# A two-layer graph network: x kept in SBUF and updated in place, dense loops laid out anew, sums cleared by GpSimd, shorter one-hot and destination rings

## The chip, the cores and the metric

One core of one Trainium2 chip runs the whole program. The metric is device time in microseconds of one execution. The kernel before has a median of 10818.31 us over 3 runs (10810.28 to 10887.77). The profile of one execution shows what lies between its first and its last instruction.

## What is computed

There are 12500 nodes with 128 features each and 200000 edges sorted by destination, with 16 features per edge. Three steps over the edges follow one another, each with a step over the nodes before and after it.

```python
h = jnp.maximum(_layernorm(x, axis=-1), 0.0)
x = x + _L0_gnn_ref(h, L0_gnn_W1, L0_gnn_w2, src, dst)       # pooling: e = (tanh(h @ W1.T) @ w2)[src], softmax over dst
h = jnp.maximum(_layernorm(x, axis=-1), 0.0)
x = x + _L1_gnn_ref(h, edge_index, edge_attr_16, ...)         # two transformer convolutions
# transformer_conv(x, src, dst, edge_attr, Wq, bq, ...)
q, k, v = x @ Wq + bq, x @ Wk + bk, x @ Wv + bv
e = edge_attr @ We
alpha = jnp.sum(q[dst] * (k[src] + e), axis=-1) / jnp.sqrt(C)
p = jnp.exp(alpha - segment_max(alpha, dst)[dst])
w = p / (segment_sum(p, dst)[dst] + 1e-16)
out = segment_sum((v[src] + e) * w, dst) + (x @ Ws + bs)
```

The first convolution has 8 heads of 16 and is followed by a relu, the second has one head of 128.

## The kernel before

The nodes are padded to 98 tiles of 128 rows, and the stages over the nodes work on 14 batches (`BATCHES`) of 7 tiles (`ROWS_B`). The edges form 391 blocks of 512. A block whose edges end in several node tiles is visited once for each tile, which gives 488 items. The stages run one after another, with a barrier between them:

- `prepare` builds identities, masks and the list of items. Its last steps need a row that goes to DRAM and comes back (`row_scratch`, `end_p`).
- `hidden_stage` computes relu(layernorm(x)) and the pooling scores and writes `pool_rows`. It loads x into the buffer `acc`, four batches ahead.
- `dense_stage("pool")` is the first pass over the edges. GpSimd gathers the rows of the source nodes, four gathers per block, into a ring of 8 blocks, and VectorE adds the weighed sums to `acc` in SBUF.
- `project_stage` adds the pooled sums to x, normalizes it, multiplies by the four weights at once (512 columns) and stores keys and values, skip rows and the queries split in three bf16 parts. It reads x again from DRAM into `xb` (three buffers) and writes the new x to `x1_rows`.
- `edge_stage("multi")` is the second pass over the edges (ring of 4 blocks). Its buffers `onehot` and `onehotT`, `dst` and `attr` hold 8 items (`U`), and the queries hold 4 (`QB`).
- `fold_stage` finishes the first convolution and prepares the second. It reads `skip1_rows` and `x1_rows` and writes `h2_rows`, `skip2_rows` and `query_cols`. The query is computed in two products, by Wq and then by a folded key weight.
- `dense_stage("single")` is the third pass over the edges.
- `output_stage` multiplies the sums by Wv and by the 17 rows of edge weights and bias, divides, adds `skip2_rows` and stores the output.

Each of the three passes begins with VectorE clearing `acc`, which is 128 x 14355 words. `acc` and `run_max` stay in SBUF all the time.

The order of the work is written out by hand. Each engine has a program of its own, and the engines wait for each other's semaphores. `D_["hidden"].wait(pe, n)` makes TensorE wait until batch n of h is there. `rolled` writes the steps of a loop out in full. In `project_stage`, `fold_stage` and `output_stage` TensorE transposes a batch, waits until ScalarE has copied the result to SBUF (`turned_sb`), and multiplies the same batch. Below, T stands for the seven transposes of a batch, and M for its products.

## Time and profile before

| | us |
|---|---|
| median of 3 runs | 10818.31 |
| span of the profiled execution | 7414.1 |
| difference of the two | 3404.2 |
| prepare and hidden_stage | 192 |
| first pass over the edges | 1986 |
| project_stage | 296.4 |
| second pass | 2367.6 |
| fold_stage | 278.5 |
| third pass | 2079.5 |
| output_stage | 214 |

The profile gives no time of its own for the profiled execution beyond the span from its first to its last instruction. The stages are cut at the first instruction that belongs to each.
### The profile page before, as it was taken

The numbers are of one execution on the slowest core, as the hardware profiler recorded it, in microseconds if no ns is written. First come the engines' busy times: TensorE is split into PE (matmuls) and PEld (weight loads), VectorE is DVE, ScalarE is ACT, GpSimd is POOL, SyncE is SP. The second block draws the span as 40 slices with busy tenths as digits, with TensorE's granted clock in tenths as the row PEclk, the third lists the DMA queues.
The fourth block names the chain that finished last, engine by engine and source line by source line (L and its number), as shares of the span: only waits on it lengthen the run. The fifth ranks groups of instructions, "written<-read, shape, count | busy, mean of one in ns | idle before, by whom it ended". The sixth has DMA issues, their size and how long they took to land. (4 is left out here: it accounts for less than half of the span.)

```text
span 7414.1 us, 172328 instructions
## 1 busy us (share of the span) xinstructions
PE 5718.3 (77%) x38285; PEld 4085.0 (55%) x38285; DVE 4663.7 (63%) x12926; ACT 3438.6 (46%) x8180; POOL 4576.5 (62%) x4707
## 2 busy tenths in 40 slices
PE   4555566666665688888888888856889999999998
PEld 3455555555542466666666666633555556666666
DVE  4444555555665788999999999933444555555542
ACT  3233333333443466666666666612444444444441
POOL 0777777777750477777666665502777777777630
PEclk7777878888986799999999999977999999999995
DMA  2334444444434666666655555534445555555532
GB/s 81 85 82 83 85 85 87 88 89 89 92 90 140 161 155 157 159 158 153 151 144 145 142 140 137 130 103 119 108 110 112 117 116 119 123 122 123 119 88 60
DMA packets 1267854, 861.45 MB, mean 116 GB/s; under 512 B 637234, under 2 KB 1158320, under 8 KB 1266840
## 3 DMA queue, kind: packets, MB, share of 16 engines
q1 hardware_dynamic: 1091672, 438.53, 25.3%
...
HBM read 780.46 MB, written 69.42 MB: 115 GB/s over the span
## 5 line engine op out<-in xcount | busy, mean ns | idle before, releaser
L757 POOL DMA_INDIRECT ring_multi<-kv_rows,src_cols x1564 | 1609.3, 1029 | 1029.7 <-issue 440.4
L1155 POOL DMA_INDIRECT ring_single<-h_rows,src_cols x1564 | 1482.6, 948 | 857.2 <-issue 480.3
L1155 POOL DMA_INDIRECT ring_pool<-pool_rows,src_cols x1564 | 1482.0, 948 | 678.6 <-issue 451.5
L1258 PE MATMUL ps_s_pool<-ident,row_pool 128*128 128x128 f32 x1952 | 365.1, 319 | 718.0 <-ACT row_pool L1300 716.8
L1300 ACT ACTIVATE row_pool<-ring_pool 128x520 f32 x488 | 309.1, 633 | 1162.1 <-POOLq L1146 1162.1
L958 PE MATMUL ps_e_multi<-w_edge,attrT 64*128 64x512 f32 x976 | 544.5, 638 | 331.4 <-DVE kv L847 310.9
L1222 DVE CUSTOM_DVE_ANT_0 masked_pool<-mask_pool,ps_s_pool,start_pool 128x512 f32<-128x512 bf16 x488 | 364.8, 748 | 633.4 <-PE ps_s_pool L1258 552.3
L1271 PE MATMUL ps_p_pool<-row_pool,probT_pool 128*128 128x129 f32 x3904 | 667.1, 325 | 55.2 <-DVE probT_pool L1235 54.2
L847 DVE TENSOR_TENSOR kv<-ring_multi,ps_e_multi 128x1024 f32<-128x1024 f32 x488 | 596.1, 1222 | 161.6 <-issue 124.0
L1258 PEld LDWEIGHTS ps_s_pool<-ident,row_pool 128*128 128x128 f32 x1952 | 254.1, 160 | 801.5 <-issue 764.9
L1305 ACT ACTIVATE rowT<-ps_r 128x512 f32<-128x512 f32 x488 | 291.7, 598 | 816.4 <-PE ps_r L1265 816.4
L1271 PEld LDWEIGHTS ps_p_pool<-row_pool,probT_pool 128*128 128x128 f32 x3904 | 602.7, 235 | 97.5 <-DVE probT_pool L1235 97.2
L1222 DVE CUSTOM_DVE_ANT_0 masked_single<-mask_single,ps_s_single,start_single 128x512 f32<-128x512 bf16 x488 | 364.7, 747 | 427.8 <-PE ps_s_single L1253 424.3
L948 PE MATMUL ps_p_multi<-message_multi,onehot 128*128 128x136 f32 x3904 | 584.2, 297 | 0.5 <-issue 0.4
L1271 PE MATMUL ps_p_single<-row_single,probT_single 128*128 128x145 f32 x3904 | 581.1, 292 | 2.4 <-DVE probT_single L1235 2.4
L1253 PE MATMUL ps_s_single<-edge_tail,cols_tail 17*128 17x512 f32 x976 | 549.7, 643 | 0.0
L948 PEld LDWEIGHTS ps_p_multi<-message_multi,onehot 128*128 128x128 f32 x3904 | 536.7, 207 | 0.9 <-issue 0.7
L1271 PEld LDWEIGHTS ps_p_single<-row_single,probT_single 128*128 128x128 f32 x3904 | 525.2, 194 | 3.6 <-DVE probT_single L1235 2.8
L1251 PE MATMUL ps_s_single<-rowT,cols 128*128 128x512 f32 x976 | 512.2, 607 | 1.5 <-issue 1.5
L1230 DVE SCALAR_TENSOR_TENSOR acc<-acc,factor_single,ps_p_single 128x145 f32 x488 | 178.9, 367 | 521.0 <-PE ps_p_single L1271 513.4
L1265 PEld LDWEIGHTS ps_r<-ident,row_single 128*128 128x128 f32 x1952 | 207.9, 142 | 493.1 <-issue 255.7
L1300 ACT ACTIVATE row_single<-ring_single 128x512 f32 x488 | 304.2, 623 | 294.5 <-POOLq L1146 292.0
...
## 6 DMA issues: line engine op xcount, KB each, us to landing
dst_pool<-in_dst_rows SPq DMA_DIRECT2D x488, 128.0 KB
dst_multi<-in_dst_rows SPq DMA_DIRECT2D x488, 128.0 KB
dst_single<-in_dst_rows SPq DMA_DIRECT2D x488, 128.0 KB
query_multi<-query_parts SPq DMA_DIRECT2D x488, 96.0 KB
cols<-query_cols SPq DMA_DIRECT2D x488, 64.0 KB
ring_pool<-pool_rows,src_cols POOLq DMA_INDIRECT x1564
ring_multi<-kv_rows,src_cols POOLq DMA_INDIRECT x1564
ring_single<-h_rows,src_cols POOLq DMA_INDIRECT x1564
```

The costliest lines, as they stand in the source:

```text
L757: pool.indirect_dma_start(out=ring[:, u, j, :], out_offset=None, in_=rows, in_offset=bass.IndirectOffsetOnAxis(ap=g.src_cols[:, c:c + 1], ...
L847: V.tensor_tensor(out=kv[:, u1 % 4], in0=in_ring(items.block(m1), 0, 2 * D).rearrange("p j (a c) -> p j a c", a=2), in1=ps_e[:].rearrange( ...
L948: i = T_.matmul(ps_p[:, 0:acc_w], lhs, rhs, start=(j == 0), stop=(j == J - 1))
L958: T_.matmul(ps_e[:], attrT[:, u % 2], w_edge[:].rearrange("k j c -> k (j c)"), start=True, stop=True).then_inc(E["edge"].sem, 1)
L1155: pool.indirect_dma_start(out=ring[:, u, j, :], out_offset=None, in_=rows, in_offset=bass.IndirectOffsetOnAxis(ap=g.src_cols[:, c:c + 1], ...
L1222: V.tensor_tensor_reduce(out=masked[:, p], in0=mask[:, p], in1=ps_s[p][:], scale=1.0, scalar=start[:, p], op0=ALU.add, op1=ALU.min, accum_ ...
L1251: T_.matmul(ps_s[p1][:], cols[:, u1 % QB], rowT[:, p1], start=True, stop=False)
L1253: T_.matmul(ps_s[p1][:], cols_tail[:, u1 % QB], edge_tail[:, u1], start=False, stop=True)\
L1258: i = T_.transpose(ps_s[p1][:, j * P:(j + 1) * P], row[:, u1, j, D + 1:D + 2].to_broadcast([P, P]), g.ident[:])
L1271: i = T_.matmul(ps_p[p3][:, 0:acc_w], probT[:, p3, j], row[:, u3, j, 0:acc_w], start=(j == 0), stop=(j == J - 1))
L1300: S_.activation(row[:, u, :, 0:copied], in_ring(items, u, 0, copied), ACT.Copy)\
L1305: S_.activation(rowT[:, u % 2], ps_r[u % 2][:], ACT.Copy).then_inc(E["rowT_sb"].sem, 1)
```

## The change

- x is loaded once, in `prepare`, into a new buffer `x_rows` that keeps all 98 tiles in SBUF. The 14 loads stand on the sync engine's queue ahead of the stores and loads of `row_scratch`. `project_stage`, `fold_stage` and `output_stage` update it in place. The loads of x and of `x1_rows` and `skip2_rows` and the stores to these two are gone. The output is stored from `x_rows`.
- GpSimd clears `acc`: all of it in `hidden_stage`, and batch by batch (1015 words per partition) in `project_stage` and `fold_stage`, as soon as VectorE has read the sums. VectorE's clear at the start of each pass is gone.
- In the three node stages TensorE now transposes batch n before it multiplies batch n - 1, and the transposed batch has two buffers. VectorE prepares batch n + 1 before it evacuates batch n - 1.
- In `fold_stage` Wq and the folded key weight are multiplied once, ahead of the loop, so that a batch's product by Wq alone and the copy `qT` between the two are gone. Skip rows are loaded up to three batches ahead.
- In `output_stage` the seven tails of 17 columns are transposed together (119 columns), and the second product of each tile takes all 119 rows with a weight matrix that is zero outside its own 17 rows. The products go to two PSUM buffers of a batch each, and semaphores count batches where they counted tiles.
- In the second pass `onehot` and `onehotT` hold 6 items (`OB`) and `dst` holds 4.
- `dst_cols`, which nothing read, and its transposes in `prepare` are gone.

The core of the diff:

```diff
+OB = 6
...
+        g.x_rows = sb(g, ctx, "x_rows", [P, NODE_TILES, D])
+        g.x_loaded = [sem(g, f"x_loaded{k}") for k in range(BATCHES // 2)]
...
+            for n in range(BATCHES):
+                sp.dma_start(g.x_rows[:, n * ROWS_B:(n + 1) * ROWS_B], rows_of(t["x"], n)).then_inc(g.x_loaded[n // 2], 16)
...
+        @block.gpsimd
+        def _(pool):
+            pool.memset(g.acc[:], 0.0)
...
-            for n in range(BATCHES):
-                D_["stats"].wait(sp, n - LOADS)
-                sp.dma_start(acc[:, n * ROWS_B:(n + 1) * ROWS_B, 0:D], rows_of(t["x"], n))\
-                  .then_inc(loaded[n % LOADS], 16)
...
-        onehot = sb(g, ph, f"onehot_{kind}", [P, U, J, P], BF16)
-        onehotT = sb(g, ph, f"onehotT_{kind}", [P, U, J, P], BF16)
+        onehot = sb(g, ph, f"onehot_{kind}", [P, OB, J, P], BF16)
+        onehotT = sb(g, ph, f"onehotT_{kind}", [P, OB, J, P], BF16)
...
-            dst = sb(g, ph, "dst_multi", [P, U, EDGES_B], U16)
+            dst = sb(g, ph, "dst_multi", [P, QB, EDGES_B], U16)
...
-                    E["rel"].wait(sp, n - U)
-                    sp.dma_start(dst[:, u], t["dst_rows"][ds(b, 1), :].to_broadcast([P, EDGES_B]))\
+                    E["rel"].wait(sp, n - QB)
+                    sp.dma_start(dst[:, u % QB], t["dst_rows"][ds(b, 1), :].to_broadcast([P, EDGES_B]))\
...
-            V.memset(g.run_max[:], -BIG)
-            V.memset(g.acc[:], 0.0).then_inc(g.acc_clear, 1)
+            V.memset(g.run_max[:], -BIG).then_inc(g.acc_clear, 1)
...
-                    E["edge_max"].wait(act, n - U)
-                    S_.activation(onehotT[:, u].rearrange("p j n -> p (j n)"), apart[:, u % 2], ACT.Relu,
+                    E["edge_max"].wait(act, n - OB)
+                    S_.activation(onehotT[:, n % OB].rearrange("p j n -> p (j n)"), apart[:, u % 2], ACT.Relu,
                                   scale=-1.0, bias=one[:]).then_inc(E["onehotT_sb"].sem, 1)
...
@@ project_stage @@
+        @block.gpsimd
+        def _(pool):
+            for n in range(BATCHES):
+                D_["x_sum"].wait(pool, n)
+                pool.memset(acc[:, n * ROWS_B:(n + 1) * ROWS_B, :], 0.0)
+            pool.memset(acc[:, NODE_TILES:SLOTS, :], 0.0)
...
+            def summed(n):
+
+                u = n % 2
+                sums = acc[:, n * ROWS_B:(n + 1) * ROWS_B, :]
+                V.tensor_scalar(den[:, u].unsqueeze(2), sums[:, :, D:D + 1], 1e-30, None, ALU.max)\
+                 .then_inc(D_["den"].sem, 1)
+                D_["den"].wait(dve, n)
+                V.reciprocal(den[:, u], den[:, u]).then_inc(D_["extra"].sem, 1)
+                D_["extra"].wait(dve, n)
+                for j in range(ROWS_B):
+                    x1 = xr[:, n * ROWS_B + j]
+                    i = V.scalar_tensor_tensor(out=x1, in0=sums[:, j, 0:D], scalar=den[:, u, j:j + 1], in1=x1,
+                                               op0=ALU.mult, op1=ALU.add)
+                i.then_inc(D_["x_sum"].sem, 1)
...
+            summed(0)
...
+                if has(k - 1, BATCHES):
+                    rest(k - 1, 0)
+                if has(n + 1, BATCHES):
+                    summed(n + 1)
+                if has(k - 1, BATCHES):
+                    rest(k - 1, 1)
...
         def _(pe):
             pe.wait_ge(s_wdve, 1)
-            for n in range(BATCHES):
-                D_["hidden"].wait(pe, n)
-                D_["turned_sb"].wait(pe, n - 1)
-                for j in range(ROWS_B):
-                    i = T_.transpose(ps_h[:, j], h[:, n % 2, j], ident[:])
-                i.then_inc(D_["turned"].sem, 1)
-                D_["turned_sb"].wait(pe, n)
-                for j in range(ROWS_B):
-                    i = n * ROWS_B + j
-                    evac.wait(pe, i - 6)
-                    T_.matmul(ps_z[i % 6][:], hT[:, j], w[:].rearrange("p a n -> p (a n)"),
-                              start=True, stop=True).then_inc(D_["product"].sem, 1)
+            for n in range(BATCHES + 1):
+                if has(n, BATCHES):
+                    D_["hidden"].wait(pe, n)
+                    D_["turned_sb"].wait(pe, n - 1)
+                    for j in range(ROWS_B):
+                        i = T_.transpose(ps_h[:, j], h[:, n % 2, j], ident[:])
+                    i.then_inc(D_["turned"].sem, 1)
+                k = n - 1
+                if has(k, BATCHES):
+                    D_["turned_sb"].wait(pe, k)
+                    for j in range(ROWS_B):
+                        i = k * ROWS_B + j
+                        evac.wait(pe, i - 6)
+                        T_.matmul(ps_z[i % 6][:], hT[:, k % 2, j], w[:].rearrange("p a n -> p (a n)"),
+                                  start=True, stop=True).then_inc(D_["product"].sem, 1)
 
...
@@ fold_stage @@
-            def step(n, u):
-                D_["hidden"].wait(pe, n)
-                D_["turned_sb"].wait(pe, n - 1)
-                for j in range(ROWS_B):
-                    i = T_.transpose(ps_h[:, j], h[:, u, j], ident[:])
-                i.then_inc(D_["turned"].sem, 1)
-                D_["turned_sb"].wait(pe, n)
-                D_["query_done"].wait(pe, n - 1)
-                for a, b in halves:
-                    i = T_.matmul(flat(ps_q, a, b), wq[:], flat(hT, a, b), start=True, stop=True)
-                i.then_inc(D_["q_turned"].sem, 1)
-                D_["product_read"].wait(pe, n - 1)
-                for j in range(ROWS_B):
-                    i = T_.matmul(ps_z[:, j], hT[:, j], ws[:], start=True, stop=True)
-                i.then_inc(D_["product"].sem, 1)
-                D_["q_turned_sb"].wait(pe, n)
-                for a, b in halves:
-                    T_.matmul(flat(ps_c, a, b), folded[:, 0:D], flat(qT, a, b), start=True, stop=True)
-                    i = T_.matmul(flat(ps_q, a, b)[0:TAIL], folded[:, D:ACC_W], flat(qT, a, b), start=True, stop=True)
-                i.then_inc(D_["folded"].sem, 1)
-            rolled(pe, BATCHES, 2, 0, step)
+            T_.matmul(ps_q[:, 0:2].rearrange("p a n -> p (a n)")[:, 0:ACC_W], wqT[:], folded[:], start=True, stop=True)
...
+            for n in range(BATCHES + 1):
+                if has(n, BATCHES):
+                    D_["hidden"].wait(pe, n)
+                    D_["turned_sb"].wait(pe, n - 1)
+                    for j in range(ROWS_B):
+                        i = T_.transpose(ps_h[:, j], h[:, n % XB, j], ident[:])
+                    i.then_inc(D_["turned"].sem, 1)
+                k, v = n - 1, (n - 1) % 2
+                if has(k, BATCHES):
+                    D_["turned_sb"].wait(pe, k)
+                    D_["q_turned_sb"].wait(pe, k - 1)
+                    for a, b in halves:
+                        i = T_.matmul(flat(ps_q, a, b)[0:TAIL], both[:, D:ACC_W], flat(hT[:, v], a, b), start=True, stop=True)
+                    i.then_inc(D_["q_turned"].sem, 1)
+                    D_["query_done"].wait(pe, k - 1)
+                    for a, b in halves:
+                        i = T_.matmul(flat(ps_c, a, b), both[:, 0:D], flat(hT[:, v], a, b), start=True, stop=True)
+                    i.then_inc(D_["folded"].sem, 1)
+                    D_["product_read"].wait(pe, k - 1)
+                    for j in range(ROWS_B):
+                        i = T_.matmul(ps_z[:, j], hT[:, v, j], ws[:], start=True, stop=True)
+                    i.then_inc(D_["product"].sem, 1)
...
@@ output_stage @@
-        sT = sb(g, ph, "sT", [P, ROWS_B, P])
-        tT = sb(g, ph, "tT", [TAIL, ROWS_B, P])
+        sT = sb(g, ph, "sT", [P, 2, ROWS_B, P])
+        tT = sb(g, ph, "tT", [TAILS, 2, P])
...
+            for j in range(ROWS_B):
+                sp.dma_start(wt[j * TAIL:j * TAIL + EDGE_DIM, j], t["L1_gnn_We1"]).then_inc(s_w, 16)
+                sp.dma_start(wt[j * TAIL + EDGE_DIM:(j + 1) * TAIL, j], row_of(t["L1_gnn_bv1"])).then_inc(s_w, 16)
...
+                    for j in range(ROWS_B):
+                        T_.transpose(ps_h[:, j], acc[:, n * ROWS_B + j, 0:D], ident[:])
+                    T_.transpose(ps_t[n % 2][0:TAILS, 0:P], tail[:, n % 2].rearrange("p t c -> p (t c)"), ident[:])\
+                      .then_inc(D_["turned"].sem, 1)
+                k, v = n - 1, (n - 1) % 2
+                if has(k, BATCHES):
+                    if k == 0:
+                        pe.wait_ge(s_w, 16 * (1 + 2 * ROWS_B))
+                    D_["turned_sb"].wait(pe, k)
+                    evac.wait(pe, k - 2)
+                    for j in range(ROWS_B):
+                        T_.matmul(ps_z[v][:, j], sT[:, v, j], wv[:], start=True, stop=False)
+                        i = T_.matmul(ps_z[v][:, j], tT[:, v], wt[:, j], start=False, stop=True)
+                    i.then_inc(D_["product"].sem, 1)
```

VectorE in the middle of `project_stage`, before (`den`, `xb`, `stat`, `agg` belong to the sums and the layernorm of a batch, `parts` and `out` to the queries and the evacuated products):

```order
L1423 SCALAR_TENSOR_TENSOR xb<-acc,den,xb 128x128 [waits dense_extra,x_loaded1]
L1423 SCALAR_TENSOR_TENSOR xb<-acc,den,xb 128x128 x6
L1428 BN_STATS stat<-xb 128x6 [waits dense_x_sum]
L1428 BN_STATS stat<-xb 128x6 x6
L1432 BN_AGGR agg<-stat 128x2 [waits dense_stats]
L1432 BN_AGGR agg<-stat 128x2 x6
L1409 TENSOR_TENSOR out<-out,parts 128x7x128 [waits dense_part]
L1438 RECIPROCAL rstd<-std 128x7 [waits dense_std]
L1441 SCALAR_TENSOR_TENSOR drift<-agg,rstd 128x7 [waits dense_hidden,dense_rstd]
L1448 TENSOR_TENSOR out<-ps_z,b_qkvs 128x512 [waits dense_product,kv_stored0]
L1448 TENSOR_TENSOR out<-ps_z,b_qkvs 128x512 [waits dense_product] x6
L1409 TENSOR_TENSOR out<-out,parts 128x7x128 [waits dense_part]
```

and in the changed kernel:

```order
L1426 SCALAR_TENSOR_TENSOR drift<-agg,rstd 128x7 [waits dense_hidden,dense_rstd]
L1415 TENSOR_TENSOR out<-out,parts 128x7x128 [waits dense_part]
L1392 TENSOR_SCALAR den<-acc 128x7
L1395 RECIPROCAL den<-den 128x7 [waits dense_den]
L1399 SCALAR_TENSOR_TENSOR x_rows<-acc,den,x_rows 128x128 [waits dense_extra]
L1399 SCALAR_TENSOR_TENSOR x_rows<-acc,den,x_rows 128x128 x6
L1404 BN_STATS stat<-x_rows 128x6 [waits dense_x_sum]
L1404 BN_STATS stat<-x_rows 128x6 x6
L1408 BN_AGGR agg<-stat 128x2 [waits dense_stats]
L1408 BN_AGGR agg<-stat 128x2 x6
L1415 TENSOR_TENSOR out<-out,parts 128x7x128 [waits dense_part]
L1439 TENSOR_TENSOR out<-ps_z,b_qkvs 128x512 [waits dense_product,kv_stored2]
```

The wait for the load of x is gone, and the summing of the next batch stands between the scale of one batch and the evacuation of the batch before it.

TensorE in the middle of `fold_stage`, before:

```order
L1625 MATMUL ps_h<-ident,h 128x128 [waits dense_turned_sb,dense_hidden]
L1625 MATMUL ps_h<-ident,h 128x128 x6
L1630 MATMUL ps_q<-hT,wq 128x512 [waits dense_query_done,dense_turned_sb]
L1630 MATMUL ps_q<-hT,wq 128x384
L1634 MATMUL ps_z<-ws,hT 128x128 [waits dense_product_read]
L1634 MATMUL ps_z<-ws,hT 128x128 x6
L1638 MATMUL ps_c<-qT,folded 128x512 [waits dense_q_turned_sb]
L1639 MATMUL ps_q<-qT,folded 17x512
L1638 MATMUL ps_c<-qT,folded 128x384
L1639 MATMUL ps_q<-qT,folded 17x384
```

and in the changed kernel:

```order
L1654 MATMUL ps_h<-ident,h 128x128 [waits dense_turned_sb,dense_hidden]
L1654 MATMUL ps_h<-ident,h 128x128 x6
L1661 MATMUL ps_q<-hT,wq_folded 17x512 [waits dense_q_turned_sb,dense_turned_sb]
L1661 MATMUL ps_q<-hT,wq_folded 17x384
L1665 MATMUL ps_c<-hT,wq_folded 128x512 [waits dense_query_done]
L1665 MATMUL ps_c<-hT,wq_folded 128x384
L1669 MATMUL ps_z<-ws,hT 128x128 [waits dense_product_read]
L1669 MATMUL ps_z<-ws,hT 128x128 x6
```

Between the transposes of a batch and the product that needs them now stand the products of the batch before, and the two products from `qT` are gone.

TensorE in the middle of `output_stage`, at the change from the transposes to the products, before:

```order
L1740 MATMUL ps_h<-ident,sums 128x128
L1741 MATMUL ps_tail<-ident,sums 17x128
L1746 MATMUL ps_z<-wv,sT 128x128 [waits dense_product_read,dense_turned_sb]
L1747 MATMUL ps_z<-wt,tT 128x128
L1746 MATMUL ps_z<-wv,sT 128x128 [waits dense_product_read]
L1747 MATMUL ps_z<-wt,tT 128x128
```

and in the changed kernel:

```order
L1762 MATMUL ps_h<-ident,acc 128x128 [waits dense_turned_sb,dense_acc_read]
L1762 MATMUL ps_h<-ident,acc 128x128 x6
L1763 MATMUL ps_tail<-ident,sums_tail 119x128
L1772 MATMUL ps_z<-wv,sT 128x128 [waits dense_product_read,dense_turned_sb]
L1773 MATMUL ps_z<-wt,tT 128x128
L1772 MATMUL ps_z<-wv,sT 128x128
```

The single transposes of the tails have become one, the transposes read `acc` itself, and the wait before each tile's products stands once in a batch.

## Rows read from the trace of the kernel before

**Rows 1.** Windows: PE, PEld, DVE, ACT, POOL busy (count), PEclk, DMA share, GB/s.

```profile
0.00:192.00 192.00, 76.78 (x339) 63.35 (x339) 91.39 (x484) 56.61 (x118) 2.46 (x15) 0.71 0.29 82
192.00:2178.00 1986.00, 1216.67 (x7808) 1090.44 (x7808) 1078.37 (x2930) 709.74 (x1465) 1482.03 (x1564) 0.84 0.41 86
2178.00:2474.40 296.40, 147.87 (x294) 64.48 (x294) 153.09 (x481) 94.56 (x169) 0.00 (x0) 0.68 0.47 143
2474.40:4842.00 2367.60, 1981.00 (x19032) 1451.11 (x19032) 2137.07 (x5860) 1544.89 (x4393) 1609.32 (x1564) 0.95 0.60 147
4842.00:5120.50 278.50, 145.10 (x464) 77.78 (x464) 78.48 (x102) 49.28 (x56) 0.00 (x0) 0.71 0.41 120
5120.50:7200.00 2079.50, 1968.11 (x9760) 1209.04 (x9760) 1077.14 (x2930) 959.65 (x1952) 1482.64 (x1564) 0.98 0.53 115
7200.00:7414.00 214.00, 182.81 (x588) 128.80 (x588) 48.13 (x141) 23.87 (x28) 0.00 (x0) 0.53 0.21 61
```

**Rows 2.** The timeline in project_stage; start us, us, engine, operation [idle before].

```profile
2195.19 1.73 PE L1460 MATMUL ps_h<-ident,h 128*128 128x128 f32 x7 [18.50 <-ACT h L1494]
2197.92 8.62 PE L1466 MATMUL ps_z<-w_qkvs,hT 128*128 128x512 f32 x14 [1.01 <-ACT hT L1502]
...
2308.18 0.95 ACT L1480 ACTIVATE parts<-out 128x896 bf16<-128x896 f32 x1 [1.16 <-DVE out L1409]
...
2321.72 2.80 ACT L1494 ACTIVATE h<-xb,drift,rstd 128x128 f32<-128x128 f32 x7 [0.99 <-DVE drift L1441]
...
2316.37 1.93 DVE L1423 SCALAR_TENSOR_TENSOR xb<-acc,den,xb 128x128 f32<-128x128 f32 x7 [7.91 <-DMA xb<-in_x]
...
2463.29 0.36 SPq L1385 DMA_DIRECT2D kv_rows<-out  x1
```

**Rows 3.** The timeline in fold_stage, TensorE and VectorE.

```profile
4866.29 0.99 PE L1625 MATMUL ps_h<-ident,h 128*128 128x128 f32 x7
4869.96 1.74 PE L1630 MATMUL ps_q<-hT,wq 128*128 128x512 f32 x4 [2.69 <-ACT query_tail L1658]
4871.54 1.72 PE L1634 MATMUL ps_z<-ws,hT 128*128 128x128 f32 x14
...
4889.26 3.29 PE L1630 MATMUL ps_q<-hT,wq 128*128 128x512 f32 x4 [2.69 <-ACT query_tail L1658]
...
4880.97 0.25 DVE L1585 TENSOR_SCALAR den<-acc 128x56 f32<-128x56 f32 x1 [16.83 <-DMA x<-x_rows]
...
4885.68 1.08 DVE L1610 TENSOR_TENSOR x<-x,ps_z 128x896 f32<-128x896 f32 x1
```

**Rows 4.** The timeline in output_stage, TensorE.

```profile
7267.19 0.79 PE L1746 MATMUL ps_z<-wv,sT 128*128 128x128 f32 x2 [1.79 <-ACT tT L1757]
...
7268.63 0.80 PE L1746 MATMUL ps_z<-wv,sT 128*128 128x128 f32 x2
...
7386.16 0.49 PE L1746 MATMUL ps_z<-wv,sT 128*128 128x128 f32 x2 [1.79 <-ACT tT L1757]
...
7386.99 0.49 PE L1746 MATMUL ps_z<-wv,sT 128*128 128x128 f32 x2
```

**Rows 5.** The timeline of VectorE at the start of the second edge stage.

```profile
2478.78 12.02 DVE L814 MEMSET acc<- 128x14355 f32 x1 [2.94 <-issue]
2491.20 1.22 DVE L847 TENSOR_TENSOR kv<-ring_multi,ps_e_multi 128x1024 f32<-128x1024 f32 x1 [0.40 <-DVE acc L814]
```

**Rows 6.** The timeline in prepare, GpSimd and VectorE.

```profile
2.09 0.50 POOL L265 MEMSET fresh_row<- 1x488 f32 x1
...
31.84 1.62 DVE L335 TENSOR_SCALAR passed<-iota_f,end_p 98x488 f32<-98x488 f32 x4
```

**Rows 7.** The window while hidden_stage loads x.

```profile
52.00:54.00 2.00, 0.47 (x1) 0.18 (x1) 0.43 (x2) 0.00 (x0) 0.00 (x0) 0.50 1.13 319
```

**Rows 8.** The timeline at the end of the second edge stage.

```profile
4809.78 0.35 SPq L793 DMA_DIRECT2D dst_multi<-in_dst_rows  x1
...
4819.05 0.72 ACT L1012 ACTIVATE apart_multi<-dst_multi,node_ids 128x512 f32<-128x512 uint16 x1
```

416 lines of the change are left out of this document (191 added, 225 removed).

## The prediction

> **What bounds the kernel now.** I read the windows by stage first, since a share over the whole span mixes stages with different limits. [rows 1] The three passes over the edges take 6433 of 7414 us. In the first, GpSimd's gathers are busy 1482 of 1986 us, TensorE 61%; the ring is filled at GpSimd's pace. In the second VectorE is busy 90% of the time. In the third TensorE is busy 95% at a clock of 0.98. The three stages between them are different: in project_stage, fold_stage and output_stage, 789 us together, VectorE is busy for about half the time or less, and the DMA share is 0.21 to 0.47. These stages wait. The timelines say for what. In project_stage VectorE waits 7.91 us for a load of x in each batch [rows 2], in fold_stage up to 16.83 us for the load of x1 [rows 3], and in output_stage TensorE stands 1.79 us in each batch until ScalarE has copied the transposed sums, and runs at a clock of 0.53 though it is busy 85% of the time [rows 1, 4]. The gain has to come from these 789 us. In the passes the change can only win or lose something at the start, or in the rings.
>
> The median of the runs is 3404 us above the span. The profile does not show what lies there. I take it as constant: predicted time = 10818 minus what the span loses.
>
> **project_stage.** Now: 296.4 us [rows 1]. The load is gone, so what is late next? In the new order evacuating batch k - 1 on VectorE is followed by ScalarE's first part of the queries (0.95), by its seven activations for batch k + 1 (2.80), by T on TensorE (1.73), by M of batch k (8.62 for 14 passes), and by the last evacuation (0.7, an estimate from VectorE's 153.09 us of work); with 0.1 to 0.2 us at each hand-over that is 15.0 us [rows 2]. The two TensorE terms are from a batch after a long idle time. If TensorE stays warm, T costs 0.99 and M 6.5 (four passes over 2 x 896 columns took 1.74, so 14 passes of 512 columns take 14 x 0.46) [rows 3], and the period is 12.3. VectorE has some 10.9 us of work in a batch (153.09 / 14) [rows 1], so it does not bind. TensorE's idle time in the new period is about 4.8 us; after 2.69 us of idle the same product took 1.74 us once and 3.29 us another time [rows 3]. I take 14. The first batch's M started at 2197.92, 20 us into the stage; now it stands behind T of batch 1, which comes 4.6 us later, so batch 0 is evacuated at 20 + 4.6 + 8.6 + 0.7 = 34 us. Then 12 periods of 14 = 168, the last M without a T before it 7, and from the last evacuation (the store at 2463.29) to the end 11 us as now. Sum 220, so **76 us less**. Ends: 12.3 gives 97 less; 17 (hand-overs and a late clock together) gives 40 less.
>
> **fold_stage.** Now: 278.5 us. TensorE's work in a batch, warm: T 0.99, the tail 1.74, the main product 1.74, the skip product 1.72, together 6.2 [rows 3]; the third query product is gone. VectorE's in a batch lasts from 4880.97 to 4886.76, 5.8 us [rows 3]. The skip rows are loaded two batches ahead, and one batch moves 1.44 MB (three transfers of 459 KB and one of 61 KB); at the 319 GB/s that the load of x reached [rows 7] that is 4.5 us. So three things lie close together, TensorE last, and nothing in the loop waits for a store that it has just issued. I take 6.8 a batch. The first two batches run at half clock: 1.73 + 3.29 + 3.29 and 1.72 lengthened to about 2.8, 11.1 each. Weights, the extra product ahead of the loop and the first hidden batch put T of batch 1 at about 15 us (estimate, from 5.8 us of VectorE's work and the weights' landing as now). The last store lands some 7.5 us after the last product. 15 + 22 + 12 x 6.8 + 7.5 = 126, so **152 us less**. Ends: 6.2 a batch gives 159 less; a TensorE at half clock throughout gives 15 + 14 x 11.1 + 7.5 = 178, 101 less.
>
> **output_stage.** Now: 214 us, 15.2 a batch. Four passes take 1.44 us at half clock and 0.83 us at full clock, 0.36 and 0.208 a pass [rows 4]. In fold_stage 14 passes of the same size took 1.72 us, 0.123 a pass [rows 3]. The difference is that here passes with 128 rows of weights alternate with passes with 17. With 119 rows I expect both to be loaded alike and the price of fold_stage: 28 x 0.123 + 8 transposing passes x 0.14 = 4.6 a batch at full clock, 8.0 at half. VectorE's 3.4 a batch (48.13 / 14) [rows 1] and ScalarE's copies hide under it. The first M waits for 15 small loads, of which the sync engine issues one in about 0.4 us [rows 2], so it starts at about 9.3. 9.3 + 2 x 8.0 + 12 x 4.6 + 5 for the last evacuation and store = 85.5, **128 us less**. The clock is the open question: it was 0.53 at 85% busy. But these passes streamed their 128 columns in 0.21 of 0.36 us, and half of them used 17 rows; the third pass, with dense work, has 0.98 [rows 1]. Ends: half clock throughout, 9.3 + 14 x 8.0 + 5 = 126, 88 less; half clock with the dear passes, 9.3 + 14 x 12 + 5 = 182, 32 less.
>
> The Trainium skill ("TensorE: Matmul & The Clock Gate", Part 3, What overlaps and what doesn't) says that a weight load overlaps running matmuls only when the row group differs. By that rule 119 rows would still conflict with 128. The trace disagrees so far: fold_stage's passes all have 128 rows and cost 0.123 [rows 3], those that change between 128 and 17 cost 0.208 [rows 4].
>
> **The clears.** VectorE's clear takes 12.02 us on record at the start of each pass [rows 5]. In the first pass the gathers set the pace from the first one on, and they do not wait for VectorE: nothing gained. The third pass begins the same way: nothing. In the second VectorE is the bound and its first real work started 0.40 us after the clear [rows 5]; the data it needs is ready some 3 us earlier, so **3 us less** (between 0 and 12). GpSimd's own clears, at 0.50 us for 488 words [rows 6], take 1.04 us for a batch and 15 us for all of `acc`; GpSimd is otherwise idle in these stages [rows 1]. If VectorE stood still for each of them, that would be 28 x 1.04 + 15 = 44 us.
>
> **prepare.** The 14 loads of x, 6.4 MB, take 20 us at 319 GB/s [rows 7], and the row that goes to DRAM and back now queues behind them. VectorE used the returned row at 31.84 [rows 6]; with loads from 9 us to about 31 it comes at about 38. hidden_stage gets 1 us back, since x is already there. **5 us more** (between 1 less and 20 more).
>
> **The rings.** On the sync engine the wait for `dst` (4 items back) comes after the wait for the queries, which is also 4 items back and comes later in ScalarE's and TensorE's order. So `dst` was in fact issued 4 ahead already: the last one went out at 4809.78 and was used at 4819.05 [rows 8]. The one-hots are last read three items after they are written, and 6 slots leave three more. Nothing.
>
> **Sum.** 76 + 152 + 128 + 3 - 5 = 354 us. Span 7414 - 354 = 7060, time 10818 - 354 = **10464**.
>
> **Rivals.**
> (a) TensorE stays at half clock in the three stages. For it: output_stage's 0.53. Against: fold_stage's products of 512 columns did run at full clock in one of its batches [rows 3]. Project 64 less, fold 101, output 88, with 3 and -5 that is 251: 10567.
> (b) The 119-row passes stay dear at full clock: 28 x 0.208 + 1.1 = 6.9 a batch, 24 a batch for the two cold ones together, 121 in all, 35 us worse: 10499.
> (c) VectorE is locked out while GpSimd clears: 44 us worse, 10508. No row shows GpSimd and VectorE side by side in such stages. The Trainium skill ("SBUF — State Buffer", Who interferes with whom) says that copies and scalar operations in their fast form and a GpSimd instruction block each other wholly. By it fold_stage would suffer most, because VectorE is nearly the bound there.
> (d) What lies outside the span is not constant but grows with the span (10818 / 7414 = 1.46): 354 x 1.46 = 517 less, 10301.
> (e) Slower: six one-hot slots are too few, and ScalarE's two activations for the next item (0.72 each [rows 8]) come to stand behind TensorE's last reading instead of beside it: 488 x 1.44 = 703 us more, 10464 + 703 = 11167. It turns the sign from 0.73 us an item on (354 / 488). Against it: the three items of slack, some 14 us at 4.9 us an item.
>
> **How the numbers follow.** Forecast 0.55, (a) 0.18, (b) 0.08, (c) 0.07, (d) 0.07, (e) 0.02, and 0.03 for a gain that the unseen 3404 us swallow. About 1% is what a measurement of this kernel can tell from no change. The best of the stage ends are 97 + 159 + 133 + 3 + 1 = 393, 10425; I go on to 10390 toward (d). At the other end (a) with project_stage at its worst and 20 us in prepare makes 40 + 101 + 88 - 20 = 209, 10609; I take 10620. This leaves out (d), (e), the swallowed gain and a tenth of the rest. All but (e) and the swallowed gain are faster by over 1%: 0.95, within 1% 0.03, slower 0.02.
>
> **What would show each step.** project_stage near 220 us with a period of 12 to 15 and no DMA as a releaser on VectorE; fold_stage near 126 with TensorE busy over 85% and a clock above 0.9; output_stage near 86, its passes at 0.12 us; the memset gone from VectorE; prepare and hidden_stage near 197; the three passes within 10 us of now. I am wrong if a node stage shows half clock, if its stores hold up VectorE, or if the second pass moves by more than 20 us.

## The result and the profile after

| | runs | median, us | range |
|---|---|---|---|
| before | 4 | 10814.3 | 10789.0 to 10887.8 |
| changed | 4 | 10518.6 | 10499.7 to 10561.6 |

The ratio is 0.971, with a 95% interval of 0.967 to 0.975: 296 us less, and from the interval 269 to 356. The prediction was 10464, 354 less.

The first surprise is the span. The profiled execution of the changed kernel took 10499.7 us and its span is 10497.8, so next to nothing lies outside. These are its windows by stage, in the order and with the columns of [rows 1]: prepare and hidden_stage, first pass, project, second pass, fold, third pass, output.

```profile
0.00:203.60 203.60, 77.13 (x326) 62.94 (x326) 95.28 (x472) 56.48 (x118) 14.51 (x16) 0.71 0.29 78
203.60:3150.60 2947.00, 1353.02 (x7808) 1217.99 (x7808) 1057.75 (x2928) 699.76 (x1464) 1477.30 (x1564) 0.71 0.26 58
3150.60:3364.90 214.30, 126.98 (x294) 62.96 (x294) 159.43 (x481) 94.49 (x169) 13.38 (x15) 0.73 0.44 138
3364.90:7075.20 3710.30, 2619.19 (x19032) 1957.85 (x19032) 2217.94 (x5859) 1539.47 (x4393) 1522.05 (x1564) 0.72 0.37 94
7075.20:7188.80 113.60, 85.96 (x415) 51.28 (x415) 78.28 (x104) 39.85 (x42) 13.38 (x15) 0.90 0.60 180
7188.80:10394.60 3205.80, 2504.89 (x9760) 1500.62 (x9760) 1058.52 (x2930) 951.65 (x1952) 1476.96 (x1564) 0.80 0.32 75
10394.60:10497.80 103.20, 67.30 (x504) 64.25 (x504) 33.79 (x141) 15.20 (x28) 0.00 (x0) 0.90 0.23 64
```

Read it in two halves. The three stages over the nodes went from 296.4, 278.5 and 214.0 us [rows 1] to 214.3, 113.6 and 103.2. The three passes, which the change hardly touches, seem to have grown from 6433 to 9863 us. In the first pass VectorE is busy 1058 us (1078 before), ScalarE 700 (710) and GpSimd 1477 (1482). TensorE is busy for longer, since its granted clock is lower: 1968 us became 2505 in the third pass (clock 0.98, now 0.80), and 1981 became 2619 in the second (0.95, now 0.72) [rows 1]. The node stages show no such loss of clock (0.73, 0.90 and 0.90 here). In the third pass 537 of the 1126 us that it grew by are TensorE's own, and the rest are waits. Here is what ended the waits of one line of the first and third pass (VectorE adding the sums to `acc`), in us and times. The largest part ends in "remote", a release that the profile does not see.

```profile
  remote: 1114.7, 204
  PE ps_p_single L1265: 343.0, 246
  issue: 238.0, 126
  PE ps_p_pool L1265: 173.5, 195
```

A comparison of two profiles must first ask whether they were taken under the same conditions. The experiments answer that.

Now the node stages. In project_stage (the timeline of TensorE) a batch takes 13.66 us, from one T to the next; TensorE waits 4.46 us before T for ScalarE's h.

```profile
3239.82 1.75 PE L1451 MATMUL ps_h<-ident,h 128*128 128x128 f32 x7 [4.46 <-ACT h L1489]
3241.36 7.66 PE L1459 MATMUL ps_z<-w_qkvs,hT 128*128 128x512 f32 x14
...
3253.48 1.75 PE L1451 MATMUL ps_h<-ident,h 128*128 128x128 f32 x7 [4.46 <-ACT h L1489]
```

In fold_stage, again in TensorE's timeline, the third line of [rows 3] stands again, at 1.72 us, and nothing is left in front of it but 0 to 1 us of waiting for VectorE's h. A batch takes 5.7 to 6.8 us.

```profile
7135.76 0.98 PE L1654 MATMUL ps_h<-ident,h 128*128 128x128 f32 x7 [0.94 <-DVE h L1609]
7136.68 1.68 PE L1661 MATMUL ps_q<-hT,wq_folded 128*17 128x512 f32 x4
7138.28 1.77 PE L1665 MATMUL ps_c<-hT,wq_folded 128*128 128x512 f32 x4
7139.89 1.72 PE L1669 MATMUL ps_z<-ws,hT 128*128 128x128 f32 x14
```

VectorE's timeline says why h is late: in the second half of the loop VectorE itself waits for the load of the skip rows, 9.0 us in 8 batches.

```profile
7161.05 1.09 DVE L1607 TENSOR_TENSOR h<-h,skip 128x896 f32<-128x896 f32 x1 [1.10 <-DMA skip<-skip_rows]
```

In output_stage the products with 119 rows follow one another at 0.11 to 0.12 us a pass (two passes from 10465.12 to 10465.35), where [rows 4] had 0.208. But there is a new wait of 2.25 us in 12 of the 14 batches, on VectorE's copy of the tails.

```profile
10464.19 0.99 PE L1762 MATMUL ps_h<-ident,acc 128*128 128x128 f32 x7 [2.25 <-DVE sums_tail L1735]
...
10465.12 0.39 PE L1772 MATMUL ps_z<-wv,sT 128*128 128x128 f32 x2
10465.35 0.39 PE L1773 MATMUL ps_z<-wt,tT 119*128 119x128 f32 x2
...
10470.66 1.76 PE L1762 MATMUL ps_h<-ident,acc 128*128 128x128 f32 x7 [2.25 <-DVE sums_tail L1735]
```

### The profile page after: what moved, and what is told of

Read it like the earlier page. It is cut to its first block and busy times, and to the rows that moved or that the text cites. A ratio compares the mean times of both kernels' runs of the same rounds, so it can differ in the third digit from the quotient of the medians.

```text
span 10497.8 us, 171974 instructions
## 1 busy us (share of the span) xinstructions
PE 6834.5 (65%) x38139; PEld 4917.9 (47%) x38139; DVE 4701.0 (45%) x12914; ACT 3396.9 (32%) x8166; POOL 4517.6 (43%) x4738
## 5 line engine op out<-in xcount | busy, mean ns | idle before, releaser
L953 PE MATMUL ps_e_multi<-w_edge,attrT 64*128 64x512 f32 x976 | 739.1, 847 | 829.2 <-ACT attrT L1033 502.5
L1285 ACT ACTIVATE prob_pool<-masked_pool,low_pool 128x512 f32<-128x512 f32 x488 | 352.2, 722 | 2222.4 <-DVE low_pool L1216 1905.9
L1265 PE MATMUL ps_p_single<-row_single,probT_single 128*128 128x145 f32 x3904 | 738.2, 344 | 259.6 <-DVE probT_single L1229 213.9
L1265 PEld LDWEIGHTS ps_p_single<-row_single,probT_single 128*128 128x128 f32 x3904 | 662.7, 237 | 290.6 <-DVE probT_single L1229 238.8
L943 PE MATMUL ps_p_multi<-message_multi,onehot 128*128 128x136 f32 x3904 | 765.5, 359 | 1.3 <-issue 1.2
L943 PEld LDWEIGHTS ps_p_multi<-message_multi,onehot 128*128 128x128 f32 x3904 | 727.1, 269 | 1.1 <-issue 1.0
L1224 DVE SCALAR_TENSOR_TENSOR acc<-acc,factor_pool,ps_p_pool 128x129 f32 x488 | 170.4, 349 | 1164.2 <-remote 901.0
L953 PEld LDWEIGHTS ps_e_multi<-w_edge,attrT 64*128 64x128 f32 x976 | 183.1, 233 | 970.0 <-ACT attrT L1033 790.4
L989 PE MATMUL ps_q_multi<-query_multi,onehotT_multi 128*128 128x128 bf16 x5856 | 578.3, 272 | 0.0
L1229 DVE COPY probT_single<-ps_t_single 128x512 f32<-128x512 f32 x488 | 336.2, 689 | 439.1 <-remote 353.3
```

The costliest lines, as they stand in the source:

```text
L943: i = T_.matmul(ps_p[:, 0:acc_w], lhs, rhs, start=(j == 0), stop=(j == J - 1))
L953: T_.matmul(ps_e[:], attrT[:, u % 2], w_edge[:].rearrange("k j c -> k (j c)"), start=True, stop=True).then_inc(E["edge"].sem, 1)
L989: i = T_.matmul(ps_q[:, j], onehotT[:, n % OB, j], query[:, u % QB, k, 0:D], start=(k == 0), stop=(k == 2))
L1229: V.tensor_copy(probT[:, p1].rearrange("p j n -> p (j n)"), ps_t[p1][:])\
L1265: i = T_.matmul(ps_p[p3][:, 0:acc_w], probT[:, p3, j], row[:, u3, j, 0:acc_w], start=(j == 0), stop=(j == J - 1))
L1285: S_.activation(prob[:, p2], masked[:, p2], ACT.Exp, bias=low[:, p2], scale=-1.0)\
```

## The experiments

All twelve runs, in the order in which they ran. They fell on three chips, and the chip turned out to matter more than any edit.

**The kernel before, once more.** No edit.

> The kernel before, unchanged, profiled once more. The earlier profile of it had a span of 7414 us, while its runs take 10818 us; the profile of the changed kernel has a span of 10497.8 us for a time of 10499.7 us, so nothing lies outside the span there. Theory A: the 3404 us lie inside the three passes over the edges, and the stages over the nodes are as in the profile at hand: project_stage 296 us, fold_stage 278, output_stage 214, prepare and hidden_stage 192, each within 5 us, the three passes together about 9830 us instead of 6433. Theory B: everything is stretched alike, by 1.46: project_stage 432, fold_stage 406, output_stage 312. Theory C (the one in the prediction): span 7414 again, and the rest outside it.

Measured: 7410.4 us for the whole execution, with a span of 7408.6. Seven further runs on this chip have a median of 7403.9. Its first pass and project_stage:

```profile
191.10:2175.10 1984.00, 1228.09 (x7808) 1098.96 (x7808) 1082.21 (x2930) 709.56 (x1464) 1480.77 (x1564) 0.83 0.40 86
2175.10:2470.70 295.60, 146.47 (x294) 64.11 (x294) 152.90 (x481) 94.59 (x169) 0.00 (x0) 0.68 0.47 143
```

None of the three theories had it: the span is again near 7414, as in C, but nothing lies outside. The 7414 us were the time of the kernel on a chip like this one, and the 10818 us that of another chip.

**TensorE's order of before in the three node stages.**

```diff
 # TensorE, in project_stage; the same in fold_stage and output_stage
-                k = n - 1
+                k = n
                 if has(k, BATCHES):
                     D_["turned_sb"].wait(pe, k)
```

> The changed kernel with TensorE's order of before in the three stages over the nodes: the products of batch n follow the transposes of batch n, behind ScalarE's copy of them. All the rest stays. In the changed kernel these stages last 214 us (project), 113.7 (fold) and 103.3 (output). Theory A: the order is what hides the copy. Then fold_stage gets 14 x 1.3 = 18 us longer (132), project_stage 14 x 1.3 to 2.5 = 18 to 35 us longer (232 to 249). In output_stage TensorE already waits 2.25 us a batch for VectorE's copy of the tails, which stands behind the evacuation; the old order trades it for a wait of 1.8 us for ScalarE's copies, so output_stage stays within 7 us of 103. Theory B: the gain came from the loads and products that are gone, not from the order: all three stages within 5 us of now.

Measured: 7057.9 us, ratio to before 0.953 (0.951 to 0.955). Project, fold and output:

```profile
2186.50:2386.20 199.70, 123.88 (x294) 57.25 (x294) 153.01 (x481) 90.57 (x169) 13.44 (x16) 0.81 0.47 148
4750.70:4888.70 138.00, 95.06 (x415) 53.59 (x415) 79.07 (x104) 37.85 (x42) 13.39 (x15) 0.85 0.50 148
6967.40:7056.40 89.00, 62.22 (x504) 59.17 (x504) 33.76 (x141) 15.20 (x28) 0.00 (x0) 0.93 0.26 75
```

Both theories fall in part. fold_stage gets 24 us longer: there the new order hides the copy. project_stage gets 15 us shorter and output_stage 14 to 16 us shorter: there the new order costs time. TensorE in project_stage shows why:

```profile
2288.86 1.70 PE L1451 MATMUL ps_h<-ident,h 128*128 128x128 f32 x7
2291.57 7.27 PE L1459 MATMUL ps_z<-w_qkvs,hT 128*128 128x512 f32 x12 [1.01 <-ACT hT L1497]
2300.51 1.13 PE L1459 MATMUL ps_z<-w_qkvs,hT 128*128 128x512 f32 x2 [1.67 <-DVE out L1439]
...
2303.41 5.42 PE L1459 MATMUL ps_z<-w_qkvs,hT 128*128 128x512 f32 x12 [1.01 <-ACT hT L1497]
```

M of batch n waits 1.01 us for the copy, but then it runs while VectorE is still summing. By the time VectorE evacuates, the six PSUM buffers are full, and the seven evacuations go back to back in 4.26 us. In the changed kernel M of batch n - 1 stands behind T of batch n, which waits for h. VectorE then evacuates in step with TensorE, one tile in 0.86 us. The period here is 11.84 us between the two lines shown, 11.8 to 13.5 over ten batches and 12.8 on average, not 13.66. In output_stage TensorE waits 1.17 us in a batch for ScalarE's copies in place of 2.25 for the tails, and a batch takes 5.44 us instead of 6.47.

**Three things of before, each in its own stage.** Narrow tails in output_stage, VectorE's clears, and x loaded late.

```diff
-            pool.memset(g.acc[:], 0.0)          # and GpSimd's clears in project_stage and fold_stage
+            V.memset(g.acc[:], 0.0)             # VectorE, at the start of each pass
...
-                        i = T_.matmul(ps_z[v][:, j], tT[:, v], wt[:, j], start=False, stop=True)
+                        i = T_.matmul(ps_z[v][:, j], tT[:, v, j], wt[:], start=False, stop=True)
...
+            # the 14 loads of x now stand here, behind the loads of end_p and jump_p
             sp.wait_ge(s_load, 96)
```

> The changed kernel with three things of before, each read in its own stage. (1) output_stage transposes and multiplies the 17-column tails one by one, with 17 rows of weights. Theory A (price of alternating between 128 and 17 rows, 0.208 us a pass at full clock and 0.36 at half, instead of the 0.108 and 0.21 now measured): 28 x 0.1 = 2.8 us more a batch at full clock, 4.2 at half, and dearer transposes, so 103 becomes 145 to 175 us. Theory B (the gain was only the loads and the order): within 10 us of 103. (2) VectorE clears acc at the start of each pass, GpSimd nothing. Theory A (GpSimd's clears cost VectorE nothing): project_stage and fold_stage within 3 us of 214 and 113.7, and the first product of keys in the second pass 8 to 12 us later. Rival (VectorE is locked out during a clear): both stages 13 us shorter. (3) x is loaded behind the row that goes to DRAM and back. Theory A: VectorE uses the returned row at 32 us instead of 39.6, and hidden_stage begins at 48 instead of 56.3, but waits some 4 us for its first x. Rival: the later begin was not due to the loads; it stays at 56.

Measured: 7187.4 us, ratio 0.971 (0.969 to 0.973). Second pass and output_stage, and TensorE inside the latter:

```profile
2387.00:4802.00 2415.00, 2007.70 (x19032) 1478.70 (x19032) 2138.90 (x5859) 1543.86 (x4393) 1598.75 (x1564) 0.94 0.58 144
6988.70:7179.60 190.90, 155.85 (x588) 113.86 (x588) 33.14 (x141) 23.86 (x28) 0.00 (x0) 0.60 0.12 35
```
```profile
7062.79 0.49 PE L1755 MATMUL ps_z<-wv,sT 128*128 128x128 f32 x2
7063.21 0.48 PE L1756 MATMUL ps_z<-wt,tT 17*128 17x128 f32 x2
...
7067.28 0.79 PE L1756 MATMUL ps_z<-wt,tT 17*128 17x128 f32 x2
7068.00 0.80 PE L1755 MATMUL ps_z<-wv,sT 128*128 128x128 f32 x2
```

(1) Passes that alternate between 128 and 17 rows cost 0.21 us again at full clock (0.42 for two) and 0.36 at half. output_stage becomes 191 us, worse than I expected, because its clock falls to 0.60 as well. The width of the weights, together with the joint transpose of the tails that this edit also takes back, is worth 86 of the stage's 109 us of gain. (2) Without GpSimd's clears project_stage and fold_stage stay at 214.7 and 114.5 us: they hold nobody up there. In hidden_stage it is otherwise. In the changed kernel (the first two lines, from its run on the slower kind of chip below) a multiplication on VectorE that takes 0.21 us without the clear (the third line, from this run) lasts until the clear ends, 8.08 us.

```profile
57.16 12.07 POOL L434 MEMSET acc<- 128x14355 f32 x1 [53.94 <-POOLq L197]
61.22 8.08 DVE L460 TENSOR_SCALAR w2b<-w2b 128x128 f32<-128x128 f32 x1
...
53.85 0.21 DVE L456 TENSOR_SCALAR w2b<-w2b 128x128 f32<-128x128 f32 x1
```

(3) VectorE uses the returned row at 29.6 us instead of 39.6 and hidden_stage begins at 47.3 instead of 56.3. The second pass, though, is 50 us longer than in any other kernel, which needed runs of its own.

**Two orders moved further.**

```diff
 # VectorE, output_stage
-                if has(n + 1, BATCHES):
-                    divisors(n + 1)             # copies the tails
+                if has(n + 2, BATCHES):
+                    divisors(n + 2)
 # VectorE, project_stage: rstd and drift (scale) of batch n + 1 ahead of the evacuation
+                if has(n + 1, BATCHES):
+                    scale(n + 1)
                 if has(k, BATCHES):             # evacuates batch k = n - 1
 # ScalarE, project_stage
+                if has(n + 1, BATCHES):
+                    hidden(n + 1)
                 if has(k, BATCHES):
                     part(k, 0)
```

> The changed kernel with two orders moved further. In output_stage VectorE copies the tails two batches ahead instead of one, so that the transposes no longer wait behind its evacuation. In project_stage VectorE computes scale and drift of batch n + 1, and ScalarE h of batch n + 1, ahead of the evacuation of batch n - 1. Theory A: in output_stage the 2.25 us of idle TensorE in each batch go, 103.3 becomes 74 to 80 us; in project_stage the 4.46 us of idle TensorE go and VectorE's own work of 10.9 us is the period instead of 13.66, so 214 becomes 175 to 185. Together 55 to 68 us less than the changed kernel, 0.6%. Rival: another limit is close behind (stores, ScalarE, or a clock at half), and each stage gains less than 10 us.

Measured: 7008.6 us, ratio 0.947 (0.945 to 0.949). Project and output, and VectorE and TensorE:

```profile
2191.40:2382.90 191.50, 120.92 (x294) 56.12 (x294) 152.71 (x481) 94.67 (x169) 13.40 (x15) 0.79 0.49 154
6937.50:7006.80 69.30, 60.44 (x504) 59.67 (x504) 33.76 (x141) 15.20 (x28) 0.00 (x0) 0.91 0.34 96
```
```profile
2290.82 4.27 DVE L1445 TENSOR_TENSOR out<-ps_z,b_qkvs 128x512 f32<-128x512 f32 x7
...
6962.09 0.93 PE L1775 MATMUL ps_h<-ident,acc 128*128 128x128 f32 x7
...
6966.09 0.93 PE L1775 MATMUL ps_h<-ident,acc 128*128 128x128 f32 x7
```

output_stage is 34 us shorter, more than expected: TensorE has no wait left, and a batch takes 4.00 us. project_stage is 23 us shorter, less than expected, since VectorE still waits about 1 us for ScalarE's first part of the queries in each batch.

**The changed kernel itself.**

> The changed kernel, unchanged, beside the kernel before on a chip on which that one takes about 7404 us. Theory A: the stages add up as in the runs so far: prepare and hidden_stage 203, first pass 1985, project 214, second pass 2364, fold 114, third pass 2076, output 103; 7059 us, 345 less than before, ratio 0.953. Rival: on this chip a stage is other than in the profile of 10498 us, and the sum misses by over 15 us.

This run fell on a chip on which the kernel before takes 10577 us. Measured: 10259.4 us, ratio 0.972 (0.966 to 0.977), 318 us less. The stages over the nodes are as ever, 214.5, 113.9 and 103.3 us; the passes take 2849, 3560 and 3151.

**The rings alone, in the kernel before.**

```diff
-                    E["rel"].wait(sp, n - U)
+                    E["rel"].wait(sp, n - QB)   # dst; likewise n - U to n - OB for the one-hots
```

> The kernel before with the rings of the second pass alone changed: one-hots 6 ahead instead of 8, destinations 4 instead of 8. VectorE still clears acc at its start. In the run with three things of before the second pass, with six one-hots and VectorE's clear, took 2415 us, 45 to 50 more than in the kernel before (eight, VectorE's clear: 2368 to 2371) and in the changed one (six, GpSimd's clear: 2364). Theory A (prediction): the rings cost nothing; 2370 us, ratio 1.000, and the 50 us came from something else in that kernel. Theory B: the shorter rings cost 45 us when VectorE starts late; second pass near 2415, ratio 1.006.

Measured: ratio 1.000 (0.998 to 1.003). The profile also shows where the 3404 us lie, since this is the kernel before but for the rings. First pass, project_stage and output_stage on this chip:

```profile
193.80:3066.00 2872.20, 1360.21 (x7808) 1222.18 (x7808) 1068.94 (x2930) 699.72 (x1464) 1481.15 (x1564) 0.71 0.27 59
3066.00:3361.30 295.30, 143.34 (x294) 62.93 (x294) 152.67 (x481) 94.59 (x169) 0.02 (x1) 0.69 0.47 144
10312.00:10523.30 211.30, 180.50 (x588) 127.00 (x588) 47.99 (x140) 23.86 (x28) 0.00 (x0) 0.55 0.21 62
```

project_stage takes 295 us on either kind of chip, the first pass 1984 or 2872.

**GpSimd's clears alone, in the kernel before.**

```diff
+        @block.gpsimd                           # project_stage; the same in fold_stage
+        def _(pool):
+            for n in range(BATCHES):
+                D_["x_sum"].wait(pool, n)
+                pool.memset(acc[:, n * ROWS_B:(n + 1) * ROWS_B, :], 0.0)
...
-            V.memset(g.acc[:], 0.0).then_inc(g.acc_clear, 1)
```

> The kernel before with GpSimd clearing acc batch by batch in project_stage and fold_stage, and no clear by VectorE at the start of the second and third pass. The rest, rings of eight too, stays. Theory A (prediction): the second pass loses only the 3 us of its start, 2367; the third pass loses nothing (2077); project_stage and fold_stage stay at 296 and 278 within 3 us, since VectorE is idle for half of them. Theory B: the late start throws the second pass into a longer period, so that without it the pass is some 10 us or more shorter even with rings of eight.

Measured: ratio 0.998 (0.995 to 1.001), project_stage 296.0 and fold_stage 279.3 us. The node stages agree with theory A. The second pass took 3535, 3560, 3571 and 3636 us in the four kernels profiled on this chip, so B is neither shown nor refuted.

**Both orders moved further, and x loaded behind the returned row.** The kernel of the fourth run, with the third edit of the mixed one.

> The changed kernel with the two orders moved further (tails copied two batches ahead in output_stage, scale and h one batch ahead in project_stage), and x loaded behind the row that goes to DRAM and back. The first two gave 7008.6 us. Theory A: prepare ends at 47 us instead of 56, and hidden_stage lasts 142 to 147 us, so 9 to 15 us less: 6994 to 7000. Rival: the 14 us that the mixed kernel gained in these stages came from GpSimd's clear being away from hidden_stage; then only 9 us or less are gained.

Measured: 10194.7 us, ratio 0.963 (0.957 to 0.969). Prepare and hidden_stage take 192.3 us instead of 203.4: 11 us less, as theory A has it.

**The last four, on the faster kind of chip again.** The first, second and fourth are the changed kernel, the rings alone and the kernel just described, once more.

> The changed kernel once more, hoping for a chip on which the kernel before takes some 7400 us (the last four went to one on which it takes 10577). Theory A there: the stages add up to 7059 us, 345 less than before. On a chip of the other kind: as measured, near 10260, with the stages over the nodes unchanged and only the three passes longer.

Measured: 7066.8 us beside 7405.9 for before, ratio 0.954 (0.952 to 0.956): **339 us less**, on the kind of chip on which the profile of before was taken. Its first pass and second pass are those of [rows 1] to within 4 us each:

```profile
203.20:2185.70 1982.50, 1226.47 (x7808) 1098.20 (x7808) 1067.08 (x2928) 708.93 (x1464) 1478.50 (x1564) 0.83 0.40 86
...
2400.80:4766.20 2365.40, 1986.30 (x19032) 1454.76 (x19032) 2123.71 (x5859) 1543.79 (x4393) 1615.74 (x1564) 0.95 0.60 147
```

> The kernel before with six one-hots and four destinations, once more, since on the other chip 50 us drown in the scatter of the passes. Theory A: second pass 2370 us as with eight, same time as before. Theory B (short rings and VectorE's late start together cost some 45 us): second pass near 2415, 7450 us.

Measured: 7406.5 us, ratio 1.000 (0.999 to 1.001). Second pass 2368.7 us. The rings cost nothing.

The third has VectorE's clear in the second pass alone:

```diff
-            pool.memset(acc[:, n * ROWS_B:(n + 1) * ROWS_B, :], 0.0)    # project_stage
...
-            V.memset(g.run_max[:], -BIG).then_inc(g.acc_clear, 1)
+            V.memset(g.run_max[:], -BIG)
+            V.memset(g.acc[:], 0.0).then_inc(g.acc_clear, 1)
```

> The changed kernel with one thing of before: VectorE clears acc at the start of the second pass, GpSimd no longer does in project_stage. Theory A: the clear at the start is what made the second pass 50 us longer in the mixed kernel; second pass near 2415 us, the whole near 7108. Theory B (prediction): only the 3 us of the start, 2367. project_stage stays at 214 us if GpSimd's clears do not hold VectorE up, and is 13 us shorter if they do.

Measured: 7067.5 us, the same as the changed kernel. Project_stage and the second pass:

```profile
2184.40:2398.80 214.40, 127.00 (x294) 62.97 (x294) 159.49 (x481) 94.49 (x169) 0.00 (x1) 0.73 0.44 138
2398.80:4771.10 2372.30, 1988.53 (x19032) 1460.39 (x19032) 2136.46 (x5860) 1545.37 (x4393) 1612.57 (x1564) 0.95 0.59 146
```

The clear delays VectorE's first product of keys by 2.6 us (16.75 after the stage's start, 14.19 in the changed kernel), and the pass is 7 us longer. GpSimd's clears are gone from project_stage, which stays at 214.4. This kernel has VectorE's clear and the rings of six together, as the mixed one has, and its second pass takes 2372 us. So neither the clear nor the rings, alone or together, explain the 50 us of the mixed kernel.

> The changed kernel with both orders moved further and x loaded behind the row that goes to DRAM and back, once more. On the other chip its stages over the nodes were 192, 191, 115 and 69 us, 67 us less than in the changed kernel. Theory A: 6992 to 6998 us on a chip where the changed kernel takes 7059. Rival: part of it is given back in the passes (they start in another state), as the second pass did with VectorE's clear; over 7010.

Measured: **6992.0 us**, ratio 0.944 (0.943 to 0.946), 75 us less than the changed kernel and the fastest of all. Nothing is given back:

```profile
193.20:2172.30 1979.10, 1222.69 (x7808) 1094.91 (x7808) 1066.96 (x2928) 710.19 (x1464) 1477.64 (x1564) 0.83 0.40 86
2172.30:2363.80 191.50, 120.19 (x294) 55.43 (x294) 152.93 (x481) 94.67 (x169) 13.39 (x15) 0.80 0.49 154
2363.80:4729.50 2365.70, 1989.33 (x19032) 1459.01 (x19032) 2124.39 (x5859) 1543.86 (x4393) 1605.24 (x1564) 0.95 0.59 147
```

## Why the prediction was right, and where it was not

The stages side by side, in us. "Measured" is the changed kernel beside [rows 1], on the same kind of chip.

| term | predicted gain | measured gain |
|---|---|---|
| project_stage | 76 | 296.4 - 215.1 = 81 |
| fold_stage | 152 | 278.5 - 113.6 = 165 |
| output_stage | 128 | 214.0 - 105.4 = 109 |
| start of the second pass | 3 | 2367.6 - 2365.4 = 2 |
| first and third pass | 0 | 2, from the rest of the spans |
| prepare and hidden_stage | -5 | 192 - 203.2 = -11 |
| sum | 354 | 7414.1 - 7066.4 = 348 |

The span came out at 7066 where 7060 was predicted. The ranking of the terms held. That the sum is right to 6 us is in part luck: the errors, of up to 19 us, mostly cancel.

**The premise that failed** is "3404 us lie outside the span, and are constant". Nothing lies outside. The profile was of a chip on which the kernel takes 7414 us, the times were of one on which it takes 10814, and the difference lies inside the three passes. That the subtraction survived was luck: the change works in the node stages, whose length is the same on both kinds of chip. Had it worked in the passes, the same premise would have given a wrong number. On the chips of the slower kind the gain is 296 us (269 to 356) and 318 us (245 to 359). Both intervals hold 348. Whether the passes give back some 30 to 50 us there, or the scatter between runs hides it (10521 to 10643 us for the kernel before on one such chip), the runs do not tell. Rival (d), a gain that grows by 1.46, is refuted: the node stages do not grow.

**project_stage.** I took a period of 14; it was 13.66. Right in size, but not for the reason that the change's order suggests. That TensorE idles in the new period was in the text ("about 4.8 us"); that the old order would idle less was not weighed. The first experiment puts the new order of TensorE at 15 us of loss. What gained was the load of x that is gone, with the orders of VectorE and ScalarE. No run separates these two. But VectorE's waits for that load were 88.3 us in 12 batches before, and none is left.

**fold_stage.** The loop was sized right, 6.8 against 5.7 to 6.8, but "TensorE last" was wrong for its second half: there TensorE waits 0.9 us for h and VectorE 1.1 us for the skip rows. The transfers, which I had put at 4.5 us a batch from 319 GB/s, set the period: the core moves 207 GB/s there, and the sync engine's four issues of a batch stand one behind the other for 6.7 us (2.69 us for the skip rows and 1.2 to 1.5 for each store, where a store issued at the start of the loop took 0.4). The other mis-sized term is "the first two batches run at half clock, 11.1 each": T of batch 1 came at 16.3 us into the stage (15 predicted), and the next T only 7.1 us later, since the clock rose within the first product. TensorE was busy 76% of the window, not over 85%, because the start and the last stores count in it. Of the 165 us the new order is worth 24. The loads, stores and products that are gone were not tested one by one. VectorE's waits for the load of x1 were 168.6 us in 13 batches before, and that load is gone.

**output_stage.** This is the step that failed most, by 19 us: "VectorE's 3.4 a batch and ScalarE's copies hide under it". They would, in another order. VectorE's program has the tails of batch n + 1 behind the evacuation of batch n - 1. That evacuation waits for M of batch n - 1, and T of batch n + 1 waits for the tails. TensorE therefore waits 2.25 us in 12 batches, 27 us, and the fourth run took 34 us away by moving that one copy. I had read the engine's total of work and not the place of the copy in its program. (The 133 us in the sum of the best ends is worked out nowhere in the prediction.)

**The passes with 119 rows** cost 0.11 to 0.12 us at full clock, no more than the 0.123 assumed, so rival (b) is refuted. By the rule of the Trainium skill that I quoted ("TensorE: Matmul & The Clock Gate", Part 3, What overlaps and what doesn't) their weight loads could not overlap the matmuls with 128 rows. The trace disagrees: in output_stage of the fourth run the matmuls are busy 60.4 us and the weight loads 59.7 of 69.3, so at least 50 us are both at once. Passes with 17 rows beside 128 cost 0.21 in the mixed kernel.

**The clock,** rival (a): the granted clock was 0.73 in project_stage, 0.90 in fold_stage and 0.88 to 0.90 in output_stage. Half clock throughout did not happen. In output_stage the clock moved between the two levels: T took 1.76 us in some batches and 0.99 in others.

**GpSimd's clears,** rival (c). The 44 us are refuted: the clears hold up neither project_stage (215.1 with them, 214.4 without) nor fold_stage (113.6 and 114.5). In hidden_stage the mechanism is there, which the prediction put at nothing. One scalar operation of VectorE's waits for the end of the 12.07 us clear and takes 5.2 to 8.1 us in place of 0.21, in each of the eight profiles that have the clear there. With x loaded at the same place hidden_stage lasts 145.4 and 146.5 us with the clear, 141.7 without, so it costs some 4 to 5 us. The Trainium skill ("SBUF — State Buffer", Who interferes with whom) says that copies and scalar operations in their fast form are blocked, and that an instruction with two SBUF inputs is not held up by a GpSimd instruction that only writes. The traces agree with both: in project_stage and fold_stage the clears of 0.94 us fall beside `BN_STATS` (0.3 us or less each) and beside the sum of h and the skip rows (1.09 us with and without a clear), and never beside a copy or a scalar operation. By that reading fold_stage was not the stage to suffer most.

**prepare and hidden_stage.** The mechanism was right and the size too small. The returned row was used at 39.6 us (38 predicted), but hidden_stage began 8.5 us later than before. It also lasted 147 us instead of 144, where I had expected a gain of 1: the clear held up VectorE at its start.

**The rings,** rival (e): nothing, as predicted, to within 0.1%.

**Open:** the second pass of the mixed kernel took 2415 us where all others take 2364 to 2372. Its four runs agree within 12 us, so it is no chance. It is neither the rings nor VectorE's clear. Also open is what makes the passes wait on the slower chips. Each chip appears in one series of runs, so the runs do not even tell the chip from another circumstance of that series.
